# State-space layers that sum their states by accumulating transposes, with a token-major gate

## The reference, cut to what matters

```python
h  = layernorm(x) * (1 + scale) + shift          # L3: then h = h[:, perm]
xz = h @ W_in                                    # 256 -> 1024
x_in, z = split(xz)                              # 512 channels each
u  = silu(causal_conv(x_in, conv_w, 4 taps) + conv_b)
dt_r, Bm, Cm = split(u @ W_xp)                   # 64, 16, 16
dt = softplus(dt_r @ W_dt + b_dt)
# 512 channels, 16 states each, 512 steps of time
state = state * exp(dt * A) + (dt * u) * Bm      # A = -exp(A_log)
y  = sum over the 16 states of state * Cm
y  = (y + u * D_param) * silu(z)
x  = x + gate * (y @ W_out)                      # L3: y = y[:, inv_perm]
```

## Time and profile before

| | us |
|---|---|
| median of 3 runs | 3869.78 (3867.14 to 3873.81) |
| span of the profiled execution | 3873.2 |
| busy in the span: PE / DVE / ACT / POOL | 2902.1 / 2801.5 / 2089.7 / 1716.0 |
| a batch of bodies 1 to 6, L1 / L3 | 139.5 / 153.6 |
| mean granted TensorE clock | 0.83 |

### The profile page before, as it was taken

One profiled execution on the slowest core, in us unless ns is written; L12 is line 12 of the kernel. 1 busy time (PEld: TensorE's weight loads), 2 busy tenths in 40 slices (PEclk: granted clock), 3 DMA queues, 4 the chain that ended last, 5 costly groups with the idle time before them and its releaser, 6 DMA issues. The chain is left out here.

```text
span 3873.2 us, 38272 instructions
## 1 busy us (share of the span) xinstructions
PE 2902.1 (75%) x11060; PEld 1488.6 (38%) x11060; DVE 2801.5 (72%) x3410; ACT 2089.7 (54%) x3166; POOL 1716.0 (44%) x1209
## 2 busy tenths in 40 slices
PE   6999667877777877468788878866776866867775
PEld 4555333444444444222333322223434434434443
DVE  1333279999999999755555555515999989999996
ACT  0223267777777777213444444426766756767663
POOL 0000047678677768800000000003767667677686
PEclk7899787988988988768888888768887978878888
DMA  2000111111011101043333333010101011111011
GB/s 78 11 33 22 47 39 44 39 44 50 28 44 50 50 23 55 33 82 63 60 39 66 66 61 61 12 58 33 43 24 60 30 53 50 39 45 61 23 55 49
DMA packets 101857, 176.64 MB, mean 46 GB/s; under 512 B 10219, under 2 KB 88827, under 8 KB 92563
## 3 DMA queue, kind: packets, MB, share of 16 engines
q1 hardware_dynamic: 97430, 161.65, 15.8%
q0 software_dynamic: 4224, 12.59, 1.0%
HBM read 139.69 MB, written 34.12 MB: 45 GB/s over the span
## 5 line engine op out<-in xcount | busy, mean ns | idle before, releaser
L965 POOL TENSOR_TENSOR l_h<-l_h,l_c_all 128x512 f32<-128x512 f32 x1024 | 1483.1, 1465 | 709.6 <-DVE l_h L896 688.5
L896 DVE TENSOR_TENSOR_SCAN l_h<-l_dA,l_ps_dbu 128x512 f32<-128x512 f32 x1024 | 1210.1, 1205 | 137.2 <-PE l_ps_dbu L1089 81.8
L1089 PE MATMUL l_ps_dbu<-ident,l_dub 128*128 128x128 f32 x4096 | 691.8, 303 | 282.8 <-DVE l_h L896 256.9
L767 ACT ACTIVATE l_dub<-l_duT,l_b_tok 128x512 f32<-128x512 f32 x1024 | 723.6, 711 | 281.5 <-PE l_ps_dbu L1089 281.5
L1089 PEld LDWEIGHTS l_ps_dbu<-ident,l_dub 128*128 128x128 f32 x4096 | 520.2, 154 | 783.0 <-DVE l_h L896 535.5
L781 ACT ACTIVATE l_dA<-l_dt,l_a_neg 128x512 f32<-128x512 f32 x1024 | 724.1, 711 | 0.2
L1076 PE MATMUL l_ps_y<-l_h,ident 128*128 128x512 f32 x1024 | 630.2, 702 | 104.5 <-DVE l_h L864 103.9
L1346 DVE TENSOR_REDUCE l_q_max<-l_ring 128x2 f32<-128x1024 f32 x256 | 312.7, 1224 | 335.7 <-PE l_ring L1614 332.9
L1499 ACT ACTIVATE l_probs<-l_ring 128x1024 f32<-128x1024 f32 x256 | 261.7, 1024 | 433.3 <-PE l_ring L1623 432.3
L864 DVE TENSOR_TENSOR l_h<-l_h 128x512 f32<-128x512 f32 x512 | 459.8, 901 | 26.1 <-POOL l_h L965 26.0
L925 POOL DMA_INDIRECT l_x_in<-x_dram,l_idx_x x32 | 33.2, 1038 | 951.8 <-DMA l_idx<-in_idx 938.7
(11 more groups left out here) (181 smaller groups left out, 3049.2 us busy)
## 6 DMA issues: line engine op xcount, KB each, us to landing
l_c_all<-c_rows_dram SPq DMA_DIRECT2D x64, 1024.0 KB, 4.8
l_res<-x_dram SPq DMA_DIRECT2D x24, 512.0 KB, 5.4
parts_dram<-l_parts SPq DMA_DIRECT2D x48, 256.0 KB, 2.8
l_qs<-parts_dram SPq DMA_DIRECT2D x48, 256.0 KB
l_ks<-parts_dram SPq DMA_DIRECT2D x48, 256.0 KB
l_x_in<-x_dram SPq DMA_DIRECT2D x16, 512.0 KB, 5.3
x_dram<-l_res SPq DMA_DIRECT2D x16, 512.0 KB, 3.0
su_cond_w<-in_cond_w SPq DMA_DIRECT2D x1, 5120.0 KB, 15.1
```

The lines of the kernel that those rows point to most:

```text
L767: return act.activation(dub[:, n % 2, t, :], duT[:, p, t, :], ACT.Copy, scale=b_tok[:, p, t, n:n + 1])
L896: dve.tensor_tensor_scan(h[:, h_slot(s), :], dA[:, s % DA_RING, :], ps_dbu[:, dbu_slot(s), :], 0.0, ALU.mult, ALU.add).then_inc(scan_ok, 1)
L965: pool.tensor_tensor(h[:, h_slot(s), :], h[:, h_slot(s), :], c_all[:, (n // C_GROUP) % 2, n % C_GROUP, :], ALU.mult).then_inc(hc_ok, 1)
L1089: last = pe.transpose(ps_dbu[:, dbu_slot(s), t * P:(t + 1) * P], dub[:, n % 2, t, j * P:(j + 1) * P], ident[:])
```

## The change

In both state-space layers:

- The 64 products of a batch are no longer added by DVE. PE adds each by four transposes that accumulate in `ps_y` (`sum_states`), which becomes token-major. u D is added by 16 matmuls with a diagonal tile that POOL makes once (`skip`). `h` becomes a ring of 16 slots, and POOL multiplies two of them at a time.
- The gate by silu(z) moves from POOL to DVE, which reads `ps_y` and writes over z (`silu_gate`). z is projected token-major. The result is turned back by PE and read out by ACT (`y_turn`, `y_part`) before `out_proj`.
- The convolution starts in ACT (the last tap with the bias, `conv_part`) and DVE adds the other three reading `misc` (`taps`). So `misc` is held until the third tap, and the next `x_side` waits for it.
- POOL scales the fourth token block of dt u by B in states 1 to 15.
- B is read out by ACT. Clip, max, product, exp and log of the softplus are one instruction over 2048 columns each. The layer's gate rows are loaded batch by batch.
- The places in the queues are new: layer norm at s = 0 and 1, x projections at 6, 9, 12 and 15, z at 25 to 31, `out_proj` at 34 and 48; the sums run 10 units behind, with six of them together at s = 13 to 15.

```diff
-ADD_LAG, SUM_LAG = 3, 7
+DA_RING, DBU_RING, H_RING = 8, 3, 16
+SUM_LAG = 10
+POOL_BLOCK = 3
+SUMS_AT = [[s - SUM_LAG] for s in range(UNITS)]
+SUMS_AT[SUM_LAG:SUM_LAG + 6] = [[], [], [], [0, 1], [2, 3], [4, 5]]
 # ACT
-                    if s in (17, 19, 21, 23): x_part(b, (s - 17) // 2)
-                    if s in (25, 27, 29, 31): z_part(b, p, (s - 25) // 2)
-                    if s == 32: silus(b, p)
+                    if s in (7, 10, 13, 16): conv_part(b, (s - 7) // 3)
+                    if s in (26, 28, 30, 32): z_part(b, p, (s - 26) // 2)
+                    if s == 33: silus(b, p)
+                    if s == 49: softplus(b)
+                def post_step(s, b):
+                    if s in (18, 20, 22, 24): y_part(b, (s - 18) // 2)
 # DVE
+                def taps(b, j):
+                    for i in range(TAPS - 1):
+                        k = TAPS - 2 - i
+                        back = TAPS - 1 - k
...
+                        dve.scalar_tensor_tensor(work[:, j, back:], misc[:, 0:T - back], vecs[:, c:c + 1], work[:, j, back:],
+                                                 ALU.mult, ALU.add).then_inc(cv_ok, 1)
+                def silu_gate(b, p, t):
...
+                    dve.tensor_tensor(z[:, p, t, :], ps_y[:, t, :], z[:, p, t, :], ALU.mult).then_inc(yg_ok, 1)
-                    if s == 7: ln_stats(b)
-                    if s == 10: ln_apply(b)
-                    if s in (18, 20, 22, 24): conv(b, (s - 18) // 2)
+                    if s == 0: ln_stats(b)
+                    if s == 1: ln_apply(b)
+                    if s in (8, 11, 14, 17): taps(b, (s - 8) // 3)
+                    if s == 48: clip(b)
+                    if s == 51: dt_max(b, p)
+                    if s == 52: dt_u(b, p)
-                        if s >= ADD_LAG:
-                            add_states(b, s - ADD_LAG)
 # POOL
+                def scaled(b, p, n):
+                    pool.wait_ge(dbu_ok, b * UNITS + (n - 1) * JB + CREDIT)
...
+                    pool.tensor_scalar(dub[:, n % 2, POOL_BLOCK, :], duT[:, p, POOL_BLOCK, :], b_tok[:, p, POOL_BLOCK, n:n + 1], None,
+                                       ALU.mult).then_inc(dub3_ok, 1)
+                    for q in range(H_PAIRS):
+                        if q % 2 == 0 and q // 2 + 1 < N:
+                            scaled(b, p, q // 2 + 1)
+                        if gathered and has_prep and q == 0: gather_x(b + 1)
+                        if gathered and has_post and q == 28: gather_y(b - 1, 1 - p)
...
+                        pool.tensor_tensor(two, two, c_row.to_broadcast([P, 2, T]), ALU.mult).then_inc(hc_ok, 1)
 # PE
+                def x_side(b, j):
+                    if j == 0:
+                        pe.wait_ge(mod_ok, b * DH + DH)
+                    else:
+                        pe.wait_ge(cv_ok, b * JB * (TAPS - 1) + j * (TAPS - 1))
+                def x_proj(b, p, after_post):
+                    if after_post:
+                        pe.wait_ge(og_ok, b * OUT_PARTS - 2 * OUT_PARTS + 1)
+                def y_turn(b, p, t, has_prep):
...
+                    elif has_prep:
+                        pe.wait_ge(cv_ok, (b + 3) * JB * (TAPS - 1))
-                        pe.matmul(ps_y[:, j, :], ident[:], h[:, h_slot(s0), :], start=(q < JB), stop=(n == N - 1), skip_group_check=True).then_inc(sum_ok, 1)
+                    for t in range(TB):
...
+                        last = pe.matmul(ps_y[:, t, j * P:(j + 1) * P], h[:, s % H_RING, t * P:(t + 1) * P], ident[:],
+                                         start=(s == 0), stop=(s == UNITS - 1), is_transpose=True, skip_group_check=True)
+                    if s in (6, 9, 12, 15): x_side(b, (s - 6) // 3)
+                    if s in (25, 27, 29, 31): z_side(b, (s - 25) // 2, after_post)
+                    if s == 36: x_proj(b, p, after_post)
+                    if s in (17, 19, 21, 23): y_turn(b, p, (s - 17) // 2, has_prep)
+                    if s == 34: out_proj(b, 0, has_prep)
+                    if s == 48: out_proj(b, 1, has_prep)
```

More of the change, by code:

```diff
@@ L647, in res_load @@
                     sp.dma_start(res[:], rows_of(src, b)).then_inc(res_ld, 16)
+                    sp.dma_start(gate[:], io["gates"][gate_at, bass.ds(b, 1), :].to_broadcast([P, D])).then_inc(gate_ld, 16)
                 def out(b):
@@ L680, in _ @@
                     sp.dma_start(tile[:], io[f"{L}_{name}"]).then_inc(w_ld, 16)
-                sp.dma_start(gate[:].rearrange("p b d -> p (b d)"),
-                             io["gates"][(0 if layer == 1 else 1):(1 if layer == 1 else 2), :, :].rearrange("l b d -> l (b d)").to_broadcast([P, B * D])).then_inc(w_ld, 16)
                 c_out(0, 0)
@@ L820, in ln_apply @@
                     last.then_inc(xn_ok, 1)
-                def conv(b, j):
-                    dve.wait_ge(xc_ok, b * JB + j + 1)
-                    if j == 0 and not first(b):
-                        dve.wait_ge(dt_ok, b * JB)
-                    wcol = VEC_LAYOUT[L + "_conv_w"][0] + j * TAPS
-                    dve.tensor_scalar(work[:, j, :], conv_in[:, j, 0:T], vecs[:, wcol:wcol + 1],
-                                      vec(vecs, L + "_conv_b")[:, j:j + 1], ALU.mult, ALU.add).then_inc(prep_v, 1)
-                    for k in range(1, TAPS):
-                        dve.wait_ge(prep_v, b * PREP_V + 1 + j * (TAPS - 1) + k)
-                        last = dve.scalar_tensor_tensor(work[:, j, :], conv_in[:, j, k:k + T], vecs[:, wcol + k:wcol + k + 1], work[:, j, :],
-                                                        ALU.mult, ALU.add)
-                        last.then_inc(prep_v if k < TAPS - 1 else conv_ok, 1)
@@ L860, in add_states, with clip @@
-                def add_states(b, s):
-                    if s // JB % 2:
-                        q, s0 = pair_of(s)
-                        dve.wait_ge(hc_ok, b * UNITS + s + 1 + CREDIT)
-                        dve.tensor_tensor(h[:, h_slot(s0), :], h[:, h_slot(s0), :], h[:, h_slot(s), :], ALU.add).then_inc(add_ok, 1)
+                def clip(b):
+                    dve.wait_ge(dti_ok, b * JB + JB)
+                    dve.wait_ge(u_ok, b * 2 + 1)
+                    dve.tensor_scalar(work[:], dt_in[:], 30.0, None, ALU.min).then_inc(clip_ok, 1)
@@ L911, in _ @@
             def _(pool):
-                pool.sem_inc(hc_ok, CREDIT)
+                for j in range(JB):
+                    last = pool.tensor_scalar(d_diag[:, j, :], ident[:], vec(vecs, L + "_D")[:, j:j + 1], None, ALU.mult)
+                last.then_inc(fixed_ok, 1)
                 pool.sem_inc(res_ok, CREDIT)
@@ L969, in _ @@
                 batches(pool, body)
-                for j in range(JB):
-                    silu_gate(B - 1, (B - 1) % 2, j)
                 if gathered:
@@ L1054, in out_proj @@
                         for k in range(JB):
-                            last = pe.matmul(misc[:, i * D:(i + 1) * D], y[:, k, t * P:(t + 1) * P], w_out[:, k, :], start=(k == 0), stop=(k == JB - 1))
+                            last = pe.matmul(misc[:, i * D:(i + 1) * D], y[:, t, k * P:(k + 1) * P], w_out[:, k, :], start=(k == 0), stop=(k == JB - 1))
                     last.then_inc(out_mm, 1)
                 def prep_step(s, b, p, after_post):
-                    if first(b) and s == 13:
-                        pe.wait_ge(w_ld, 16 * 5)
@@ L1061, in prep_step @@
-                    if s in (12, 14): xn_half(b, (s - 12) // 2)
-                    if s in (15, 17, 19, 21): in_proj(b, (s - 15) // 2)
-                    if s in (23, 25, 27, 29): z_proj(b, (s - 23) // 2)
-                    if s == 34: x_proj(b, p)
-                    if s == 35: b_turn(b, p)
-                    if s in (38, 40, 42, 44): dt_proj(b, p, (s - 38) // 2)
-                    if s in (53, 55, 57, 59): du_turn(b, (s - 53) // 2, after_post)
+                    if first(b) and s == 2:
+                        pe.wait_ge(w_ld, 16 * 4)
@@ new lines, in sum_states, with skip @@
+                    for t in range(TB):
+                        if s == 0 and not first(b):
+                            pe.wait_ge(yg_ok, b * TB - TB + t + 1)
+                        last = pe.matmul(ps_y[:, t, j * P:(j + 1) * P], h[:, s % H_RING, t * P:(t + 1) * P], ident[:],
+                                         start=(s == 0), stop=(s == UNITS - 1), is_transpose=True, skip_group_check=True)
+                    last.then_inc(sum_ok, 1)
+                def skip(b, j):
+                    for t in range(TB):
+                        last = pe.matmul(ps_y[:, t, j * P:(j + 1) * P], u[:, j, t * P:(t + 1) * P], d_diag[:, j, :],
+                                         start=False, stop=False, skip_group_check=True)
+                    if j == JB - 1:
+                        last.then_inc(skip_ok, 1)
```

331 lines of the change are left out of this document (177 added, 154 removed).

## The result

Three timed rounds and a profiled run gave a median of 4031.6 us (4012.5 to 4033.2) against 3871.8 for the kernel before, by as many runs: a ratio of 1.0414, 95% interval 1.0381 to 1.0448. The forecast of 3930 had the sign and little more than a third of the size: +61 us against +160. Its range ended at 4020.

A forecast was written before the change was run, and what follows sets the result against it. All four engines have 91 to 95 us a batch, so waits between them decide. Bodies 6 x 9 + 6 x 5, batch 0 -4 + 1, last batches -16 - 14, fronts 2 x 8, tail -6: +61; 3873 + 61 - 4 = 3930, range 3720 to 4020.

The forecast's parts named there:

- units 37 to 48: Loop body: PE and POOL both at 1.31 us a unit, just over the scan; 14.9 us.
- unit 0 and the wait for x: End of L1's loop body: x is loaded behind the last C rows and only unit 0's scan hides it; 12.5 us.
- The 11 us for the clock: Loop body: PE idles, drops to its lower clock level and DVE waits for the work behind; 11 us, bounds 0 and 20.
- I take 0.66, since it has one input: One POOL scaling of dt u by B, not in the trace: 0.66 us, bounds 0.66 and 1.25.
- the estimate of 0.45 to 0.6: One POOL scaling, estimated from the Trainium skill's roughly line rate for one-input work: 0.45 to 0.6 us.
- POOL's pace, 16 x 5.26 = 84: Last batch of each layer: POOL sets the pace, 84 us against 99.9 and 99.3, so -16 and -14.
- +11 a layer, less 2.8: Front part alone: four longer rounds and one-piece softplus add 11 us a layer, less 2.8 for gate rows not waited for.
- Tail of L3, where the adds waited 6.5: -6: After L3's last batch: the adds' wait of 6.5 us goes, so 6 us less.
- the clock didn't hold: Rival: PE's small work, spread over the units, keeps its clock at 2.4 GHz; 3782 us, chance 0.27.
- The scaling was dear: Rival: POOL's scaling costs 1.25 us, lengthening parts of the loop and the last batches; 3996 us, chance 0.08.
- DVE's relief: Rival: the waits overlap, so DVE's reduced work counts and a body takes 113 us; about 3500 us, chance 0.08.
- leave the clock low: Rival: transposes don't count as busy, so PE runs them slowly, some 20 us a body; 4170 us, chance 0.05.

The follow-up runs named there:

- x_early: Changed kernel with x of the batch after next fetched within the batch, not behind the last C rows or products: 1.0064 of the kernel before, 135 us less.
- xside_later: Changed kernel with the four x projections in PE's queue and ACT's first tap one unit later: 1.0186 of the kernel before, 88 us less.
- decay_lead: Changed kernel plus scale_two_input, x_early and xside_later, with ACT making exponentials three units ahead: 0.9579 of the kernel before, 78 us less than without it.
- front_banks: Changed kernel plus scale_two_input, x_early and xside_later, with three banks for the front part's projections: 0.9662 of the kernel before, 46 us less than without them.
- scale_on_act: Changed kernel with ACT scaling all four blocks of dt u by B and POOL none: 1.0253 of the kernel before, 62 us less.
- scale_two_input: Changed kernel with POOL's scaling written as a product of two tensors, B's column broadcast: 1.0209 of the kernel before, 79 us less.

## Why the forecast was wrong

The loop was right, part by part. Here is the body of L1 shown above, from its scan 1 at 979.67 to the next scan 1, against the forecast with its clock:

| part | measured | forecast |
|---|---|---|
| to the end of the first taps | 18.5 | 18.6 |
| three rounds of the taps | 27.8 | 27.4 |
| units 18 to 33 | 28.7 | 29.7 |
| wait in front of 34 | 6.45 | 6.3 |
| units 34 to 36, stop for x_proj | 8.1 | 8.0 |
| units 37 to 48 | 17.0 | 14.9 |
| softplus | 15.7 | 16.8 |
| to unit 63 | 14.7 | 14.4 |
| unit 0 and the wait for x | 11.8 | 12.5 |
| sum | 148.8 | 148.6 |

The six bodies of L1 take 147.3 to 151.2 us, those of L3 153.7 to 162.7. x_early, xside_later and decay_lead show three of these waits by taking them away. Units 37 to 48 were under-reckoned in the forecast itself: 12 units at its own 1.31 us are 15.7. In L3 the wait for x, forecast at 8 to 11 us, is 15 to 18 in five bodies of six. The 11 us for the clock were not tested as a sum. What the table of the projections shows of them is 3.5 us a body (11.2 against 7.7), where the forecast had 3.3 for the rounds.

What failed is 96 us in all:

1. **"I take 0.66, since it has one input", and the bounds 0.66 to 1.25.** A scaling took 1.57 us throughout the last batches, and up to 3.6 beside DVE's long products. Both bounds were wrong in kind: an operation on 4 elements and one with two inputs don't enclose this form, and the estimate of 0.45 to 0.6, said to lie inside them, lies below both. From it came "POOL's pace, 16 x 5.26 = 84": a block of four units took 2 x 2.35 + 1.57 = 6.3 us. The two last batches were 41 us over. The scaling makes 29 of these (2 x 16 x 0.91), the products 3, and some 9 are what a pace alone leaves out at the ends. Batch 0's 9 and the loop's 7 may hold some more of it.
2. **The front part that runs alone, "+11 a layer, less 2.8".** It came out 21 us over in the two layers. A round alone is a chain of projection at the lower level, ACT and taps:

```profile
463.02 3.65 PE L1010 MATMUL l_misc<-l_modT,l_w_in 128*128 128x512 f32 x4 [3.22 <-DVE l_work L861]
469.89 3.63 PE L1010 MATMUL l_misc<-l_modT,l_w_in 128*128 128x512 f32 x4 [3.22 <-DVE l_work L861]
```

   every 6.87 us against 2.8 before, when projections ran ahead of DVE. In L1 the taps end 11.4 us later by it, where "four rounds ... 2 us longer each" gave 8. The larger step was one left out: the gate's four projections now stand behind the taps, so from taps to clip it is 30.3 us, before 19.4, and the forecast had nothing for these 10.9. Softplus, put at 3 us longer, was shorter, 9.8 for 12.4, and hid part of the error; of the 2.8 for the gate rows nothing shows. front_banks gives all of it back, the rounds and the gate's projections together.
3. **"Tail of L3, where the adds waited 6.5: -6"**, and nothing for L1's. Measured were +5.5 and +4.2, so 16 us are missing. In L3 the adds waited for POOL's last products, behind its gathers, and the sums now wait for the same: the last product ends 11 us after the last scan, 9 before. And the way from there is longer. In L1 out_proj starts 13.6 us after the last scan, 10.7 before: gate, then four turns of y of 1.1 us, each read out by ACT before the next, stand there, 7.4 us in all. Its first half takes 6.42 us for 5.38. No run was made on this; in all runs of the changed order L3's tail stays between 54 and 56 us.
4. **The loop's and batch 0's rest**, 16 us, and 2 ahead of L1 and in L2. No cause is shown for these.

The rivals: the clock didn't hold (0.85 in L1's body). The scaling was dear, and dearer than that rival had it: its 3996 came nearest to the measured 4032, by the right term at too small a price. DVE's relief counts for a third to a half, as far as additional work can tell. Transposes do not leave the clock low: it is 0.98 as in the earlier trace rows, and 1.00 over the last batch of scale_on_act, where 539 of 603 matmuls are transposes. The Trainium skill, "TensorE: Matmul & The Clock Gate", part 4, says that a transpose doesn't count as busy for the clock in this way; the runs here don't agree, and they decide.

Open are how much the clock costs a body in all, and why scale_two_input gains 2.5 to 3 us in loop bodies where scale_on_act gains nothing (ACT's 10 us more of work would explain it; not shown).
